# Relative attention in a macaron block: scores turned by 32x32 block transposes on DVE, and values weighed for four tiles at once on 32x32 pieces of the PE array

## What is computed

```python
AC = jnp.einsum('bhid,bhjd->bhij', q + u_bias[None, :, None, :], k)
BD = jnp.einsum('bhid,hjd->bhij', q + v_bias[None, :, None, :], rp)
BD = _rel_shift(BD)
attn = jax.nn.softmax((AC + BD) * scale, axis=-1)
out = jnp.einsum('bhij,bhjd->bhid', attn, v)
```

## Time and profile before

| | |
|---|---|
| time, median of three runs | 3520.98 us (3506.55 to 3529.43) |
| span of the profiled execution | 3513.5 us |
| PE busy | 3066.5 us, 87% |
| ACT busy | 2583.4 us, 74% |
| DVE busy | 2487.6 us, 71% |
| POOL busy | 2393.8 us, 68% |
| DMA | 668.86 MB, mean 190 GB/s |

### The profile page before, as it was taken

The page is one execution under the profiler, slowest core; times in us unless marked ns, Lnnn a source line. Parts: engine busy times, 40 slices in busy tenths (PEclk is TensorE's granted clock), DMA queues, the critical chain, the costliest instruction groups (busy, mean ns, idle before and its releaser), DMA issues. The chain is left out here.

```text
span 3513.5 us, 113065 instructions
## 1 busy us (share of the span) xinstructions
PE 3066.5 (87%) x40768; PEld 2088.1 (59%) x40768; DVE 2487.6 (71%) x4784; ACT 2583.4 (74%) x4106; POOL 2393.8 (68%) x4232
## 2 busy tenths in 40 slices
PE   5565399999999999988989999999999998999965
PEld 2444166666666666666666666666666666666645
DVE  2546177787677777777868777777777776777766
ACT  2333378888788888777878888887888887888842
POOL 3224668787677878876868788777777787777720
PEclk8777599999999999999999999999999999999987
DMA  5323798998999999998999999999999999999851
GB/s 184 102 90 112 204 188 204 197 213 200 191 207 199 215 214 211 207 200 174 214 195 212 202 213 212 200 207 193 209 206 212 201 212 191 204 206 203 196 165 53
DMA packets 463823, 668.86 MB, mean 190 GB/s; under 512 B 294960, under 2 KB 386992, under 8 KB 396208
## 3 DMA queue, kind: packets, MB, share of 16 engines
q0 software_dynamic: 327680, 537.92, 71.5%
q1 hardware_dynamic: 135600, 123.75, 13.9%
HBM read 77.48 MB, written 46.14 MB: 35 GB/s over the span
## 5 line engine op out<-in xcount | busy, mean ns | idle before, releaser
L650 POOL DMA_DIRECT2D score<-to_move x4096 | 2262.0, 561 | 735.9 <-PE pt_bank L832 600.0
L889 ACT COPY to_move<-pos_bank 128x512 f32<-128x512 f32 x2048 | 1087.7, 610 | 538.5 <-PE pos_bank L765 352.5
L899 ACT ACTIVATE score<-score,low 128x1024 f32<-128x1024 f32 x1024 | 1213.5, 1186 | 20.0 <-DVE low L950 11.7
L832 PEld LDWEIGHTS pt_bank<-ident_sb,score 128*128 128x128 f32 x8192 | 965.8, 143 | 307.8 <-DVE prob_t L959 78.5
L832 PE MATMUL pt_bank<-ident_sb,score 128*128 128x128 f32 x8192 | 1129.8, 280 | 18.9 <-issue 11.7
L950 DVE CUSTOM_DVE_ANT_0 score<-ac_bank,score 128x1024 f32<-128x1024 f32 x512 | 626.9, 1224 | 651.4 <-PE ac_bank L818 582.4
L959 DVE COPY prob_t<-pt_bank 128x512 f32<-128x512 f32 x1536 | 1008.1, 684 | 7.6 <-PE pt_bank L832 6.7
L765 PE MATMUL pos_bank<-pos,qv 96*32 96x512 bf16 (+15 forms) x12160 | 651.7, 322 | 115.9 <-DMA qv<-qv_parts 51.7
L950 DVE CUSTOM_DVE_ANT_0 score<-ac_bank,score,low 128x1024 f32<-128x1024 f32 x512 | 656.5, 1282 | 129.1 <-PE ac_bank L818 108.0
L846 PE MATMUL acc_bank<-prob_t,vs 128*32 128x128 f32 x16384 | 682.1, 283 | 23.2 <-issue 23.1
L818 PE MATMUL ac_bank<-ks,qu 96*128 96x512 bf16 x2048 | 635.4, 392 | 9.4 <-DVE low L950 5.8
(11 more groups left out here) (94 smaller groups left out, 939.7 us busy)
## 6 DMA issues: line engine op xcount, KB each, us to landing
score<-to_move POOLq DMA_DIRECT2D x4096, 128.0 KB, 6.4
pos<-pos_parts SPq DMA_DIRECT2D x96, 128.0 KB, 9.2
ks<-k_parts SPq DMA_DIRECT2D x192, 64.0 KB, 7.3
qu<-qu_parts SPq DMA_DIRECT2D x768, 16.0 KB, 7.8
qv<-qv_parts SPq DMA_DIRECT2D x576, 16.5 KB, 5.1
v_heads<-v_sb SPq DMA_DIRECT2D x8, 1024.0 KB, 7.3
vs<-v_heads SPq DMA_DIRECT2D x32, 256.0 KB, 10.1
pos_parts<-part SPq DMA_DIRECT2D x16, 384.0 KB, 3.0
```

What stands on the lines that cost most here:

```text
L650: pool.dma_start(score[s::QUAD, dst:dst + FT, :], to_move[s::QUAD, src:src + FT, QUAD - 1 - s:QUAD - 1 - s + L])\
L832: last = pe.matmul(PT[c % 2][:, t * P:(t + 1) * P], lhsT=score[:, slot(k), c * BANK + t * P:c * BANK + (t + 1) * P], rhs=ident_sb[:, :], i ...
L889: act.copy(to_move[:, at + f, c * BANK:(c + 1) * BANK], ring(m)[:, :]).then_inc(pos_out, 1)
L899: act.activation(cols, cols, ACT.Exp, bias=low[:, slot(k), NH - 1:NH], scale=-1.0)\
```

## The change

DVE takes the place of PE, DVE and ACT in the turning: `turn` is now one `dve.transpose` for each half tile, 128x1024, in place in `score`. It transposes every block of 32x32 on its own, so a key's row of 32 queries then lies on a partition, but in each of the four strips of 32 partitions there are only that strip's queries. `PT`, `prob_t` and both `copy` functions are gone.

PE's `weigh` works on a whole group once its four tiles are turned. For each of 64 blocks of 32 keys and each strip r of 32 partitions it issues a matmul of 32 rows by 17 weights against 128 columns (32 queries of four tiles), so row r and column strip c mod 4 of the array; the result goes to bank r of `ACC`, which is now four banks wide. That is 256 matmuls a group, in `PIECES` = 8 parts of 32, two parts for each half of the first two steps of the next group. The position ring shrinks from three banks to two. `MADE_AT` is spread over all four steps (5, 4, 4, 4 items) in place of three (6, 6, 5). `content` stands ahead of the positions. `vs` holds every head's values four times, once for each strip; SP issues four loads for it, and four stores for each store of v in the first stage. `FIRST` is 8 in place of 4. Its core:

```diff
-            POS = [ps2(f"pos_bank{i}", BANK) for i in range(3)]
+            POS = [ps2(f"pos_bank{i}", BANK) for i in range(2)]
             AC = ps2("ac_bank", HALF)
-            PT = [ps2(f"pt_bank{i}", BANK) for i in range(2)]
-            ACC = ps2("acc_bank", FT * P)
+            ACC = ps2("acc_bank", QUADS * BANK)
...
-            MADE_AT = (range(0), range(0, 6), range(6, 12), range(12, ITEMS))
-            FOLD_AT = MADE_AT[1].stop
+            MADE_AT = (range(12, ITEMS), range(0, 4), range(4, 8), range(8, 12))
+            FOLD_AT = MADE_AT[2].stop
...
                     wait_apart(pool, pos_out, group(step, j) * ITEMS + ITEMS)
                     if there(step, FT * (j - DST)):
-                        wait_apart(pool, turned, tile(step, FT * (j - DST + 1)) * NK)
+                        wait_apart(pool, weighed, group(step, j - DST + 1) * PIECES)
...
                 def load_vs(step, h):
-                    sp.dma_start(vs[h % 2][:, :, :].rearrange("p t w -> p (t w)"),
-                                 v_heads[bass.ds(head(step, h), 1), :, :].rearrange("o p n -> p (o n)"))\
-                        .then_inc(vs_loaded[h % 2], 16)
+                    for r in range(QUADS):
+                        sp.dma_start(vs[h % 2][r * QUAD:(r + 1) * QUAD].rearrange("p c w -> p (c w)"),
+                                     v_heads[bass.ds(head(step, h), 1), :, :].rearrange("o p n -> p (o n)"))\
+                            .then_inc(vs_loaded[h % 2], 16)
...
-                    elif j or m > 2 or not isinstance(step, int):
-                        pe.wait_ge(pos_out, number - 2)
+                    elif j or m > 1 or not isinstance(step, int):
+                        pe.wait_ge(pos_out, number - 1)
...
+                def weigh(step, g, piece):
+
+                    at = g % DST * FT
+                    if piece == 0:
+                        wait_apart(pe, turned, tile(step, (g + 1) * FT) * NH)
+                        wait_apart(pe, acc_out, group(step, g) + 1)
...
+                    for c in range(piece * PIECE, (piece + 1) * PIECE):
+                        q = c % QUADS * QUAD
+                        stored = c // (TG * QUADS) * (TG * QUADS) + c % QUADS * TG + c // QUADS % TG
+                        for r in range(QUADS):
+                            rows = slice(r * QUAD, (r + 1) * QUAD)
+                            last = pe.matmul(ACC[q:q + VW, r * BANK:r * BANK + FT * QUAD], lhsT=vs[g // FT % 2][rows, stored, :],
+                                             rhs=score[rows, at:at + FT, c * QUAD:(c + 1) * QUAD],
+                                             start=(c < QUADS), stop=(c >= NBLOCK - QUADS))
                     last.then_inc(weighed, 1)
 
                 def body(step, k):
-                    n = k + POS_AHEAD
+                    n, g = k + POS_AHEAD, k // FT - 1
                     for h in range(2):
-                        if there(step, k):
-                            turn(step, k, 2 * h)
-                            turn(step, k, 2 * h + 1)
-                        weighs = k - 1 + h
-                        if there(step, weighs):
-                            weigh(step, weighs, 2 - 2 * h)
-                            weigh(step, weighs, 3 - 2 * h)
+                        weighs = k % FT < 2 and group_there(step, g)
+                        piece = k % FT * 4 + 2 * h
+                        if weighs:
+                            weigh(step, g, piece)
+                        if there(step, k + AC_AHEAD + h):
+                            content(step, k + AC_AHEAD + h, 1 - h)
                         if there(step, n):
                             for m in made_at(k, h):
                                 positions(step, n // FT, m)
-                        if h and k % FT == 1 and group_there(step, fold_no(k)):
-                            fold(step, k)
-                        if there(step, k + AC_AHEAD + h):
-                            content(step, k + AC_AHEAD + h, 1 - h)
+                        if weighs:
+                            weigh(step, g, piece + 1)
+                    if k % FT == 2 and group_there(step, g):
+                        fold(step, k)
...
+                def turn(step, k, h):
+
+                    dve.wait_ge(exped, tile(step, k) * NH + (h + 1))
+                    cols = score[:, slot(k), h * HALF:(h + 1) * HALF]
+                    dve.transpose(cols, cols).then_inc(turned, 1)
```

More of the change, by code:

```diff
@@ L821, in content @@
                     last.then_inc(ac_full, 1)
-                def turn(step, k, c):
-                    if c % 2 == 0:
-                        pe.wait_ge(exped, tile(step, k) * NH + (c // 2 + 1))
-                    if c > 1:
-                        wait_copied(pe, step, k, c - 2)
-                    elif there(step, k - 1):
-                        wait_copied(pe, step, k - 1, c + 2)
-                    for t in range(4):
-                        last = pe.matmul(PT[c % 2][:, t * P:(t + 1) * P],
-                                         lhsT=score[:, slot(k), c * BANK + t * P:c * BANK + (t + 1) * P],
-                                         rhs=ident_sb[:, :], is_transpose=True, start=True, stop=True)
-                    last.then_inc(turned, 1)
@@ L875, in _ @@
                 content(0, AC_AHEAD, 0)
-                tile_steps(pe, body, 2)
+                tile_steps(pe, body, 3)
             @block.scalar
@@ L925, in body @@
                                 take(step, n // FT, m)
[L926 to L931 removed]
                 for j in range((POS_AHEAD + 1) // FT):
[L933 removed]
+                    for m in range(MADE_AT[0].start if j == POS_AHEAD // FT else ITEMS):
                         take(0, j, m)
```

169 lines of the change are left out of this document (68 added, 101 removed).

## The result

The changed kernel takes 4685.46 us (median of 4 runs, 4680.48 to 4688.27) against 3525.2 us for the kernel before (4 runs, 3506.55 to 3547.28): 1.332 times as long, 95% interval 1.327 to 1.338. The forecast was 4374 us, its range ended at 4660. The direction was right and the size fell 311 us short. In two of three groups it is not the landing that the kernel waits for, as the forecast had it, but PE's own list of work.

A forecast was written before the change was run, and what follows sets the result against it. A loop of move, landing and last weighing part sets the group's period: 25.8 + 4.3 = 30.1 us, 6.8 more than now, 843 us over 124 groups; 10 us for the stage's end, so 4374 us, range 3900 to 4660.

The forecast's parts named there:

- The edges and the loop: Attention stage: steps from move's wait to landing's need fall from five to three, closing a loop, period 30.1 us.
- M: POOL's move of a group, from first issue until ACT goes on after its landing: 25.8 us, ends 24.0 and 27.5.
- that rival: DVE's transposes hold up POOL's DMA writing, adding 9.6 us to the issue: period 36.2 us, 5130 us; chance 0.03.
- the array pieces overlap: Rival on PE's weighing: array pieces do not overlap, period near 69 us, over 9000 us; chance 0.04.
- The short move: Rival: the move takes 22.3 us when other engines stand, period 25.7 us, 3830 us; chance 0.08.
- PE has then about 22 - 8.8 = 13 us of work in a group: PE's work per group once its 64 transposes, 8.8 us, are gone: about 13 us.
- I take 3.6 us: PE's new weighing, 512 records a group with starts 7 ns apart: 3.6 us, 0.45 us for each eighth part.
- The slower reading: PE's weighing starts at least 23 ns apart: 12 us a group, total 4505 us; a quarter of the forecast's chance.
- the tail: From landing to POOL's next move, through takes, item 3, last weighing part and POOL's reaction: 4.3 us, ends 3.0 and 4.9.
- Two passes on DVE: Rival: DVE's transpose needs two passes, 30.4 us a group, period 31 to 32 us, 4480 to 4600 us; chance 0.12.
- The ring of two banks: Two position banks: item 2 waits for item 0's take, item 3 for item 1's, a link in the loop.
- Ends of the stage: Two more steps at the attention stage's end add 10 us, an estimate.

The follow-up runs named there:

- e15: Kernel before with POOL's move waiting two tiles longer and two position banks in place of three: 4452.82 us, 1.270 times the kernel before.
- e1: Changed kernel with the second part of the weighing in each half step put ahead of the positions: 4852.4 us, 1.379 times the kernel before.
- e2: Changed kernel weighing only half of the key blocks, 256 records a group in place of 512: 4237.73 us, 1.204 times the kernel before.
- e6: Changed kernel with the weighing's operands read as bfloat16, half the records with all keys: 4197.29 us, 1.190 times the kernel before.
- e12: Kernel before with two position banks in place of three and the waits that go with them: 3733.22 us, 1.062 times the kernel before.
- e8: Changed kernel with bfloat16 weighing, all in the first step, and positions in the other three: 4263.29 us, 1.209 times the kernel before.
- e11: Changed kernel with bfloat16 weighing, all in the first step ahead of its positions, positions spread over four steps: 4215.95 us, 1.200 times the kernel before.
- e9: Changed kernel with every content matmul issued twice: 4841.62 us, 1.378 times the kernel before.
- e10: e8 with every content matmul issued twice: 4494.87 us, 1.279 times the kernel before.
- e7: Changed kernel with all eight weighing parts in the first step and positions in the other three: 5144.46 us, 1.459 times the kernel before.
- e14: Changed kernel with bfloat16 weighing and moves of half of each row: 3699.06 us, 1.055 times the kernel before.

## Why the prediction was right in direction and short in size

- **The edges and the loop: right as a mechanism, not what most groups of the changed kernel wait for.** e15 has the edges alone, T = 30.65 us, 27.0% over the kernel before, where the whole change costs 33.2%. In the changed kernel e1 takes the last part of the weighing out of the loop and nothing is won. The chain "landing, takes of items 0 and 1, items 2 and 3, last part of the weighing, next move" stands in the timeline at 2031 to 2037 us.
- **M: nearly right.** Taken from a move's first issue to its last landing, M is 24.2 us in the changed kernel and 25.6 in e15, for 25.8 with ends of 24.0 and 27.5. The issue is 17.7 us as before, 561 ns for each DMA. DVE's transposes did not hold POOL's writing up, and that rival falls; the array pieces overlap, and the transpose takes one pass, so two more fall. The short move falls too.
- **The failed step: "PE has then about 22 - 8.8 = 13 us of work in a group" and "I take 3.6 us" for the weighing.** PE is busy 24.5 us a group and halts 4.6 us more. The weighing is busy 1369.2/128 = 10.7 us. Its records start 12 ns apart at full clock and 17 ns at half, not 7 (rows below). Content and positions cost (859.1 + 918.3)/128 = 13.9 us, all by themselves more than my 13, which still held the old weighing as well. They run at a clock of 0.70; I had counted them as at 0.98. The slower reading, 12 us a group, was nearer, and I gave it a quarter of my chance. One of my signs of being wrong came with it: runs of 64 weighing records take 1.04 us (at 2035.36 us) to 1.48 us (at 2014.20, clock 0.50), and the sign was 0.8.
- **What no term had: PE's halts.** The change doubles PE's matmul records, 40,768 to 81,728. With them the instruction fetches go from 335 to 648, the halts on "issue" from 46.4 us between 1000 and 3600 us (four rows of 17.1, 14.1, 11.7 and 3.5, in 104 groups) to 380.7 (334.0, 36.7 and 10.0, in 80 groups). With the longer list between landing and next move the tail is 8.1 us and not 4.3. M + tail = 24.2 + 8.1 = 32.3 us is the period by construction, since each is measured up to where the other begins; the error is all in the tail, and M was 1.6 us shorter than forecast.
- **"Nearly every take of item 0 waits 8 to 10 us for the landing": wrong** for the changed kernel (32 takes in 105 groups, 6.1 us in the mean), nearer for e2 and e6 (7.1 us in the mean, in nearly every group). With PE's list at about 32 us, the landing is mostly there when ACT comes to it. DMA share 0.66 and 150 GB/s follow from the longer period (forecast 0.8 and 160). PE is busy 72%, not near half.
- **Sums of the forecast.** The tail's parts give 2.3 + 1.8 = 4.1 us; where the other 0.2 of its 4.3 come from is not said. Two passes on DVE would be 10.0 + 8 x 2.45 = 29.6 us, not 30.4. Neither changes the outcome.
- **The ring of two banks: right as a part of the loop, wrong as free outside it.** "The stage's other edits cost nothing" did not count what e12 shows, 6% in a kernel where the loop is not closed.
- **Ends of the stage:** 46 us, not 10. The time is wrong by T, 32.30 for 30.1 us (273 us), and by these ends (36 us).

The spacing of the starts, in a run of 68 fp32 records of the changed kernel at a granted clock of 1.00 (timeline of PE) and in one of 64 at a clock of 0.50 (duration of one in ns, minimum, median and maximum, first and last start):

```profile
2022.66 1.10 PE L826 MATMUL acc_bank<-score,vs 32*17 32x128 f32 x68
...
L826 PE MATMUL acc_bank<-score,vs x64: 388/399/416, 2014.2 to 2015.3; 32*17 32x128 f32 x64
```

The first gives (1.10 - 0.27)/67 = 12 ns with 0.27 us for the last one, the second 1.1/63 = 17 ns. Over all runs of 25 records and more between 1000 and 3300 us the medians are 12.5 and 18 ns.

The Trainium skill, "TensorE: Matmul & The Clock Gate" (Wait, 56ns, not 53.3ns?), has starts never closer than about 25 ns. These records of 32x17 pieces don't agree: 12 ns in fp32 and, in the row of e6 above, (0.43 - 0.27)/31 = 5 ns in bf16 (9 ns in the median of e6's runs). Counted by whole fp32 matmuls, of two records each, the first row comes to 25 ns, but the bf16 row, with one record a matmul, does not bear that reading out.

**What stays open.** The halts are waits for fetches and grow with what the moves load on the DMA: 4.6, 2.4 and 1.5 us a group, the longest 6.2, 2.7 and 1.9 us, for moves of 128, 64 and 8 KB. Under load the fetches start later and do not take longer. That they stand in a queue behind a move's packets fits this, but the trace does not show when a fetch was asked for, so the standing itself is not seen. Why the halts of e8 and e11 are nearly twice those of e6 with as many fetches was not tested, and what the low clock costs there was not isolated: e9 and e10 add work as they raise it. e1 is slower than the changed kernel by 1.2 us of busy time and some waits, e7 by busy time, halts and waits for ACT; why their lists cost more is not shown. None of the versions beats the kernel before; the nearest, e14, leaves half of each move out.

## What to carry to other kernels

Cost a list of small matmuls by its count of instructions as well as by array time, and at the clock that rows of a waiting engine show: here 512 small records were busy 10.7 us a group, with halts of 4.6 us beside them, where the forecast said 3.6. When a change moves a wait, look for the other wait that makes a loop with it; apart they cost 15% and 6%, together 27%. And when a profile shows "issue" idle on PE in the middle of a run of like instructions, count the packets of the instruction queue before and after, and look whether the idle ends just behind one of them.

## What was not expected of the hardware

- An fp32 matmul of 32 rows by 17 weights is two records, a bf16 one is one: 65,536 against 32,768 for the same 256 a group. Busy time for the weighing is 1369.2 us in fp32 and 453.5 us in bf16 (e6).
- PE halts inside a run of matmuls that wait for no semaphore, for up to 6.2 us with the DMA share at 0.66 and for at most 1.9 us at 0.16. It goes on 1.4 us (median) after a fetch of 16 KB is done.
- Less array work did not shorten PE's list in full: in e6 the clock fell to about 0.5, and content took 619 ns a record, against 513 in the changed kernel at 0.70 and 392 in the kernel before at 0.98.
- The transpose of 128x1024 fp32 in 32x32 blocks, in place in SBUF, takes 1.239 us, about as long as the add of as many columns.
